# A two-layer adaLN block with mixtures of experts: zeroing a scatter target piece by piece, a GpSimd drain placed ahead of ten gate operations, and two steps of the routing reordered

## What is computed

```
for layer in (0, 1):
    sa, ca, ga, sb, cb, gb = (silu(c) @ wmod) split in six, per batch element
    ga, gb = sign(g) * max(|g|, 0.25)
    x = x + ga * attn(layernorm(x) * (1 + ca) + sa)
    x = x + gb * ffn(layernorm(x) * (1 + cb) + sb)

layer 0 attn: rmsnorm, projection to 64 states, causal decaying scan, projection back
layer 0 ffn : top-1 of 8 experts, hidden 256, erf gelu, times the gate's score
layer 1 attn: 16 heads of a fast-weight recurrence over 8 chunks of 64 tokens; each chunk
              reads W_in and W_out (64 x 64 a head), then both are decayed and updated
layer 1 ffn : top-2 of 8 experts with 256 slots an expert for each choice order,
              hidden 512, tanh gelu; rows over capacity contribute nothing
```

## Time and profile before

| | us |
|---|---|
| median of 3 runs | 833.02 (831.64 to 836.5) |
| the profiled execution, own time | 835.61 |
| its span | 833.9 |
| TensorE busy | 718.4 (86%) |
| VectorE busy | 643.0 (77%) |
| ScalarE busy | 491.7 (59%) |
| GpSimd busy | 586.7 (70%) |
| mean granted TensorE clock | 0.923 |
| the chain that ended last, by engine | TensorE 71%, VectorE 9%, no releaser 7%, GpSimd 5%, ScalarE 4%, DMA 2% |

### The profile page before, as it was taken

The page is one execution under the profiler, slowest core; times in us unless marked ns, Lnnn a source line. Parts: engine busy times, 40 slices in busy tenths (PEclk is TensorE's granted clock), DMA queues, the critical chain, the costliest instruction groups (busy, mean ns, idle before and its releaser), DMA issues.

```text
span 833.9 us, 34140 instructions
## 1 busy us (share of the span) xinstructions
PE 718.4 (86%) x14802; PEld 655.3 (79%) x14803; DVE 643.0 (77%) x1057; ACT 491.7 (59%) x786; POOL 586.7 (70%) x429
## 2 busy tenths in 40 slices
PE   5577768736799999999999999999999999886997
PEld 2257567725689998988988888889988989785897
DVE  4894645527889999999988999899999999857215
ACT  4766315514675685767577666667766766637520
POOL 4243067866398989898988888888788989831750
PEclk9676659986999999999999999999999999975999
DMA  7832243411052000000000000000000000062128
GB/s 180 234 81 59 55 105 96 88 54 40 5 143 70 7 7 10 7 7 7 6 6 7 23 4 3 4 16 4 4 17 3 4 4 17 17 207 69 49 71 277
DMA packets 61598, 43.01 MB, mean 52 GB/s; under 512 B 22272, under 2 KB 54288, under 8 KB 61456
## 3 DMA queue, kind: packets, MB, share of 16 engines
q1 hardware_dynamic: 58128, 34.07, 14.7%
q0 software_dynamic: 3328, 6.82, 3.4%
HBM read 26.72 MB, written 14.16 MB: 49 GB/s over the span
## 4 chain that ended last, share of the span: by engine, by line
PE 71%; DVE 9%; issue 7%; POOL 5%; ACT 4%; DMA 2%; SPq 1%; POOLq 1%; DVEq 0%; ACTq 0%
PE psum L1875 19%; PE psum L1975 7%; PE psum L1930 7%; PE psum L1908 7%; PE psum L1966 4%; PE psum L1923 4%; PE psum L1937 4%; PE psum L1945 3%; POOL arena L561 2%; PE psum L1673 2%; PE psum L1916 2%; PE psum L2202 2%; PE psum L2226 2%; PE psum L2191 1%; PE psum L1733 1%
## 5 line engine op out<-in xcount | busy, mean ns | idle before, releaser
L1875 PE MATMUL psum<-hT,w_qkv 128*128 128x128 f32 x1408 | 173.4, 280 | 1.7 <-DVE arena L1424 1.2
L1875 PEld LDWEIGHTS psum<-hT,w_qkv 128*128 128x128 f32 x1408 | 164.0, 194 | 4.9 <-DVE arena L1424 1.4
L609 POOL TENSOR_TENSOR arena<-arena,small 128x1024 f32<-128x1024 f32 x56 | 106.0, 1914 | 50.5 <-DVE small L1437 50.5
L588 POOL TENSOR_TENSOR arena<-arena 128x1024 f32<-128x1024 f32 x56 | 106.7, 1906 | 12.4 <-ACT arena L952 12.1
L574 POOL TENSOR_TENSOR arena<-arena 128x1024 f32<-128x1024 f32 x56 | 106.6, 1903 | 0.0
L1430 DVE TENSOR_REDUCE small<-arena 128x16 f32<-128x1024 f32 x60 | 73.1, 1218 | 9.5 <-ACT arena L941 7.3
L613 POOL TENSOR_TENSOR arena<-arena 128x1024 f32<-128x1024 f32 x28 | 65.9, 2353 | 14.6 <-DVE arena L1457 14.5
L1418 DVE TENSOR_REDUCE small<-psum 128x16 f32<-128x1024 f32 x60 | 72.8, 1214 | 3.4 <-PE psum L1975 3.3
L921 ACT ACTIVATE arena<-psum 128x1024 f32<-128x1024 f32 x28 | 28.7, 1026 | 72.6 <-PE psum L1875 72.6
L561 POOL DMA_INDIRECT arena<-h_rows,route x40 | 40.3, 1008 | 43.9 <-DVE route L1275 32.0
L1424 DVE TENSOR_TENSOR arena<-psum,small 128x1024 f32<-128x1024 f32 x60 | 70.4, 1214 | 0.1
(11 more groups left out here) (325 smaller groups left out, 1651.2 us busy)
## 6 DMA issues: line engine op xcount, KB each, us to landing
y_rows<-hT SPq DMA_DIRECT2D x8, 512.0 KB, 6.4
arena<-y_rows SPq DMA_DIRECT2D x8, 512.0 KB, 7.1
o_rows<-arena SPq DMA_DIRECT2D x9, 256.0 KB, 2.4
x_sb<-in_L_attn_u SPq DMA_DIRECT2D x8, 256.0 KB, 4.4
arena<-in_W_inT SPq DMA_DIRECT2D x16, 128.0 KB
arena<-in_W_out SPq DMA_DIRECT2D x64, 32.0 KB
h_rows<-arena SPq DMA_DIRECT2D x4, 512.0 KB, 3.2
h_rows<-hT SPq DMA_DIRECT2D x8, 256.0 KB, 2.3
```

Source lines behind the costliest of these rows:

```text
L588: pool.tensor_tensor(x3, x3, lr[:, tile_of(t) * 32 + k * H:tile_of(t) * 32 + k * H + H].unsqueeze(2).to_broadcast([P, H, D]), ALU.mult).th ...
L609: pool.tensor_tensor(z4, z4, r3.unsqueeze(3).to_broadcast([P, 8, 2, CH]), ALU.mult).then_inc(done, 1)
L1875: mm = pe.matmul(ps[bank][:, p * P:(p + 1) * P], w_qkv[:, j * HD + p * P:j * HD + (p + 1) * P], hT[:, at:at + P], start=True, stop=True)
```

## The change

Four things move. The zeroing of `y_rows` becomes a function: its eight DMAs are no longer issued in a row after the first residual add of layer 1, but one behind the store of each of the first seven chunks, with two behind the first. GpSimd's drain is issued right behind the 40 gathers and ahead of the ten gate operations; the wait for the end of the phase stays behind them. VectorE computes the bfloat16 table by the comparison itself, ahead of the float32 one, in place of a cast of it. TensorE computes the modulation columns behind the 32 matmuls for the token list in place of ahead of them.

```diff
--- before.py
+++ after.py
@@ -425,8 +425,8 @@
                 sp.wait_ge(o_stored[u], 16 * (TILES0 // GRP // 2) + 16 + 16 * u)
             finish(sp, 2)
             sp.dma_start(wg1, A["L1_ffn_Wg"]).then_inc(gw, 16)
-            sp.wait_ge(x_added, 1)
-            for n in range(2 * BP):
+
+            def zero_rows(n):
                 r0 = P + n * NC * P
                 sp.dma_start(y_dram[r0:r0 + NC * P, :].rearrange("(t p) c -> p t c", p=P),
                              hT[:, T * P:(T + 1) * P].unsqueeze(1).to_broadcast([P, NC, C])).then_inc(y_zeroed, 16)
@@ -437,6 +437,9 @@
 
             for c in range(NC - 1):
                 store_rows(c)
+                zero_rows(c)
+                if c == 0:
+                    zero_rows(NC - 1)
             sp.wait_ge(x_added, T)
             sp.dma_start(b1t, A["L1_b1_cols"]).then_inc(f1_b, 16)
             sp.dma_start(b2b, A["L1_ffn_b2"].rearrange("(a e) f -> a (e f)", a=1).to_broadcast([P, E * C])).then_inc(f1_b, 16)
@@ -560,10 +563,11 @@
                 for t in range(GRP):
                     pool.indirect_dma_start(gx[g % 4][:, t * C:(t + 1) * C], None, h_dram[0][:, :], rows_of(ids_i, g * GRP + t),
                                             bounds_check=B * L - 1, oob_is_err=False).then_inc(gathered[u], 16)
+            pool.drain().then_inc(phase_end, 1)
             pool.wait_ge(mod_out, 2 * BP + 2)
             hold_gate(1, GA)
             hold_gate(1, GB)
-            finish(pool, 2)
+            pool.wait_ge(phase_end, 10)
             for n in range(4 * BP):
                 gather_back(n)
             pool.wait_ge(w_set, 16 * 80)
@@ -1231,8 +1235,8 @@
             chain.link(dve.scalar_tensor_tensor(te(pick), te(shifted), 0.0, over_t(first_w), ALU.is_equal, ALU.mult))
             dve.tensor_reduce(m2, te(pick), AX_X, ALU.max).then_inc(oh_done, 1)
             dve.wait_ge(oh_done, 1)
+            dve.tensor_tensor(te(onehot_b), te(pick), over_e(m2), ALU.is_equal).then_inc(rhs_ready, 1)
             chain.link(dve.tensor_tensor(te(onehot), te(pick), over_e(m2), ALU.is_equal))
-            dve.tensor_copy(onehot_b, onehot).then_inc(rhs_ready, 1)
             dve.tensor_copy(tile_nb, tile_no)
             dve.wait_ge(cnt_done, 1)
             before_p, totals = ps[3][:, 0:256], ps[3][:, 512:768]
@@ -1788,8 +1792,6 @@
                 if bp >= 2:
                     pe.wait_ge(mod_out, BP + bp)
                 modulation(1, bp)
-            pe.wait_ge(mod_out, 1 + 2 * BP)
-            columns(1)
             pe.wait_ge(rhs_ready, 2)
             for t in range(T):
                 if t % 8 == 0:
@@ -1797,6 +1799,8 @@
                 mm = pe.matmul(ps[2][:, 0:80], hot_of(r_hot, t), t_rhs.rearrange("p (k i s t) -> p k i s t", k=2, i=T // 8, t=8)[:, :, t // 8, :, t % 8],
                                start=(t == 0), stop=(t == T - 1))
             mm.then_inc(ids_mm, 1)
+            pe.wait_ge(mod_out, 1 + 2 * BP)
+            columns(1)
             pe.wait_ge(f0_w, 64)
             pe.wait_ge(experts_set, BP + 1)
```

## The result

Over 20 runs each the changed kernel has a median of 837.65 us, the kernel before 833.1 us. One of the changed kernel's runs, at 931.51 us and a mean granted clock of 0.721, was in a slower state and is left out of the ratio. The ratio of the runs is 1.0052, 95% interval 1.0034 to 1.0069: the changed kernel is slower, by 0.5% or 4.3 us. The forecast was 832.1 us, with a range of 829.6 to 836.6 us and a chance of 0.83 for a time within 0.5%. The profiled execution took 837.43 us (before 835.61), its span is 835.7 us.

A forecast was written before the change was run, and what follows sets the result against it. Bounds: serial VectorE/TensorE instructions up to the token list, GpSimd to layer 1's first gather, TensorE in its mixer. -0.36 and -0.5 gave -0.9 us: 834.7 us against the profiled 835.61, 832.1 on the median's scale; range 829.6 to 836.6.

The forecast's parts named there:

- The dispatch: Phase 2's start: the comparison writes the bfloat16 table itself, so TensorE's count starts earlier; gain 0.33 us, up to 0.45.
- The columns: Token list in phase 2: moving the columns gains nothing; SyncE's first result store comes 1.7 us late, at no cost.
- The drain: End of phase 2 on GpSimd: same 3.34 us behind the gathers, by a price per indirect DMA; the move gives nothing.
- first rival: Phase 2's drain waits for the last gathered rows, then pays: first gather back 3.8 us later, 835.9 us; chance 0.15.
- The third drain's end: Phase 3's drain ended at 813.66, 5.34 us behind the last scatter; 64 indirect DMAs, 0.083 us each, supporting the count price.
- The zeroing: Layer 1's mixer: old cost about 1.3 us, spread pieces cost 0.8 us, so a gain of 0.5 us.
- second rival: Chunk stores, 476 to 737 us: every piece stalls TensorE 0.98 us, eight cost 7.8 us; 839.2 us, chance 0.08.
- The sum: Whole kernel: -0.36 and -0.5 give -0.9 us, so 834.7 us profiled, 832.1 us on the median's scale.

The follow-up runs named there:

- the part alone: Kernel before with only the bfloat16 table by the comparison and the modulation columns behind the token list, drain and zeroing unmoved; ratio 0.9987 (0.996 to 1.0015).
- the padded pair: Kernel before plus eight useless operations behind GpSimd's gate operations, with the drain in its old place and moved: 851.04 and 851.23 us, ratios 1.0195 and 1.0204.
- zeroing late: Kernel before with all eight zeroing DMAs behind the load of the last experts' second weights, at about 743 us; ratio 0.996 (0.9927 to 0.9994).
- by steps: Kernel before with the zeroing in sixteen 256 KB DMAs, each behind the adding of one more tile; ratio 0.9956 (0.9929 to 0.9982).
- the one that waits and then drains: Kernel before with the drain moved behind the gathers and a wait for all 40 gathers' semaphores ahead of it; one run timed, 831.56 us beside 834.18.

## Why the prediction was wrong, step by step

- **The dispatch**: right. Forecast 0.33 us, in the trace 0.32 and 0.33 us.
- **The columns**: "moving the columns gives nothing by itself", and a first store 1.7 us late without a cost. The store was late by 3.9 us (134.59), and in the part alone the first gather back is released by SyncE and comes 0.7 us later. That is a cost of twice the dispatch's gain, which the step had at nothing. In the changed kernel it is covered, since there GpSimd is the last (0.94 <-POOL mod L539).
- **The drain**: this step failed. The price per DMA that it rested on is right and was measured three more times. The failure is in "then it costs the same 3.34 us behind the gathers: 159.91 + 3.34 = 163.25": a drain right behind the gathers did not end 3.34 us behind them, but 2.0 us behind the last packet of their rows, in all six traces that have it there. The drain ended at 166.6, and the first gather back came 2.3 us later against the last gather's end. I had this as the first rival, with 3.8 us and a chance of 0.15; the true price is between the two, as if part of the list were done while the rows are on their way. The third drain's end, 5.34 us behind the last scatter, was added from rounded times; the trace has 5.29 us. I also used rows 9, which say that the last rows are late, for a bound only.
- **The zeroing**: this step failed too, in its sign. "Shallower queues should delay less, so I take 0.8 us of new cost and a gain of 0.5 us"; the pieces cost 0.26%, about 2.2 us, on the mean of three runs. In place of the new cost of 0.8 us the traces show a stall of 2.4 to 2.6 us at the first piece and of 2.0 to 2.5 us at the third, each beside a block of instructions that starts at or just before the burst's last packet, and behind the first a clock at its lower level for 3.4 to 6.8 us. From the first to the 28th tile the traces with the pieces are 3.6 us longer on the mean. In the old place, with the same bytes in one burst of 16 us, four blocks started while it ran, and one long stall came of it (1.7 to 2.3 us in ten traces). Blocks start 3.3 to 9.1 us apart in the mixer of the kernel before, 4.3 us in the median, so not every burst of 3 us holds one up. Why a block passes in the long burst and waits in the short one is open; it fits that SyncE took 12.5 us to issue the eight DMAs there, and issued the store and the two pieces at the first place within 1.7 us. My second rival had the mechanism, with all eight pieces at 0.98 us; it was the pieces at two places, at 2.0 to 2.6 us.
- The rule of the Trainium skill (SBUF — State Buffer, "SBUF: two separate sides") that a transfer can't slow a compute instruction agrees with the traces as far as it goes: 453 matmuls took 16.75 us beside the 4 MB and 461 took 17.69 us in the next step. By that rule alone the spread would have been worth 0, where the runs show +0.26%. What came late beside the transfers was the load of instructions.
- **The sum**: +2.3 (drain) + 2.2 (zeroing) - 0.3 (dispatch) is +4.2 us, against 4.3 us measured. That it comes so near is in part luck: the zeroing's 2.2 us are known to some 1.5 us. The drain's part is shown in the trace of its path and not in a timed run of its own; the padded pair's times leave it open, and the changed kernel lost as much (1.0042) where the drain is off the path. How the 4.3 us divide is therefore not settled by timed runs.
- The chances had 0.11 for a time above 837.2 us. The first and second rival were not exclusive, and I priced each alone: a smaller form of both together is what the traces show.

## What to carry to other kernels

A drain behind indirect DMAs has a bill that grows with their number, here 0.08 us each, and right behind them a part of it is still due when the last has landed. Put it where neither matters, or leave it out where semaphores already order the work. Before bulk transfers are spread beside an engine that streams long unrolled code, look in the trace for the loads of its instructions: here bursts of 3 to 5 us held some of them up, bursts of 1 us made no long stall, and the clearest gain came from moving the transfers into a stretch in which that engine waits anyway. Two rivals that can both come true need a price for their sum.

## What the runs showed of the hardware that was not expected

- A GpSimd drain takes 0.082 to 0.084 us for each indirect DMA since the last drain: 20 and 40 DMAs gave drains of 1.69 and 3.34 us, and 64 and 104 gave ends 5.29 and 8.58 us behind the last scatter's end.
- A 16 KB block of instructions started at the last packet of the first burst ahead of it (479.33 us; the same in the four other traces with pieces), and TensorE went on 1.2 to 1.5 us behind its landing. At the third piece four of five blocks started 0.4 to 0.5 us before the last packet.
- A stall of 2.4 to 2.6 us in the mixer was followed by 3.4 to 6.8 us at the lower level of TensorE's clock in all five traces with the pieces; the five traces with the zeroing late or by steps have no such stretch from the first to the 28th tile.
- The same 40 gathers took 52 us in some sets of runs and 62 us in others, and the kernel before 833 to 835 or 868 to 871 us with them. Chip 9 stands in the record for both. No run here says why.
- The routing behind the mixer ran 3 us faster in some executions. The first 32 us behind the last tile had 0.58 of the clock in the kernel before and 0.63 in the one that waits and then drains (stretch, us, busy of each engine, PEclk, DMA share, GB/s):

```profile
735.00:767.00 32.00, 21.69 (x174) 20.63 (x173) 25.42 (x76) 16.71 (x51) 4.34 (x5) 0.58 0.54 166
```

```profile
733.90:765.90 32.00, 21.23 (x187) 20.11 (x186) 25.38 (x76) 19.55 (x61) 6.53 (x7) 0.63 0.54 168
```

The half clock lasted 30.7 us there in the first and 23.9 us in the second, behind the same work. Of the ten traces with the zeroing in its old place six have 30.7, three 27.3 and one 23.9 us; all three with it late have 23.9 us. What decides it is open; a single profiled span of this kernel can be off by 3 us for it alone.
